# The causal mask of self-attention as rows of the operands instead of mask products and masked maxima

## What is computed

```python
x = x + _L0_attn_ref(_layernorm(x), Wq, Wk, Wv, Wo)        # causal
x = x + _L0_xattn_ref(_layernorm(x), ctx, W_kv, W_q, W_proj, b_proj)
x = x + _L0_ffn_ref(_layernorm(x), gate_w, w1, b1, w2, b2)

# inside the self-attention
attn = jnp.einsum('bhqd,bhkd->bhqk', q, k) * scale
causal = jnp.triu(jnp.ones((s, s), dtype=bool), k=1)
attn = jnp.where(causal, -jnp.inf, attn)
attn = jax.nn.softmax(attn, axis=-1)
out = jnp.einsum('bhqk,bhkd->bhqd', attn, v)
```

## Time and profile before

| | us |
|---|---|
| median of 3 runs | 183.94 |
| lowest, highest | 183.62, 191.8 |
| the profiled execution | 183.63 |
| its span, first to last instruction | 181.8 |
| PE busy | 163.6 |
| DVE busy | 129.9 |
| ACT busy | 104.9 |
| POOL busy | 67.7 |
| mean granted clock of TensorE | 0.991 |
| DMA packets, MB moved | 23329, 18.39 |

### The profile page before, as it was taken

How to read it: one execution, slowest core, us unless ns; L and a number is a source line. 1 busy time by engine, 2 the same in 40 slices (tenths; PEclk the granted TensorE clock), 3 DMA queues, 4 the chain that set the end, 5 groups by cost and what they waited for, 6 DMA issues and landing times.

```text
span 181.8 us, 4434 instructions
## 1 busy us (share of the span) xinstructions
PE 163.6 (90%) x1528; PEld 117.6 (65%) x1536; DVE 129.9 (71%) x500; ACT 104.9 (58%) x218; POOL 67.7 (37%) x132
## 2 busy tenths in 40 slices
PE   5778987979899799799999999999999998989994
PEld 4457765756666577467567556656666465879983
DVE  4488599597599879879988988999955463642110
ACT  2055531257566565665567766867746766972351
POOL 6836929178900660250232232201251071124220
PEclk9999998799999999999999999999999999999999
DMA  5914254157157245134035125104402501706400
GB/s 161 286 17 127 71 157 121 50 131 184 41 143 194 64 128 151 32 101 142 24 79 159 30 78 157 32 4 123 143 7 84 177 0 26 238 29 176 118 29 29
DMA packets 23329, 18.39 MB, mean 101 GB/s; under 512 B 2308, under 2 KB 21252, under 8 KB 22660
## 3 DMA queue, kind: packets, MB, share of 16 engines
q1 hardware_dynamic: 22552, 17.20, 34.0%
q10 hardware_dynamic: 756, 0.92, 1.8%
HBM read 12.08 MB, written 2.29 MB: 79 GB/s over the span
## 4 chain that ended last, share of the span: by engine, by line
PE 55%; DVE 23%; DMA 8%; issue 5%; SPq 3%; POOL 2%; ACT 2%; DVEq 0%; POOLq 0%; ACTq 0%
PE psV L975 11%; PE psA L929 9%; PE psB L953 8%; DVE negmax L663 8%; PE psA L1019 6%; DMA stackQ<-scratch 5%; PE psV L1036 4%; PE psM L843 4%; DMA ctx_tok<-ctx_dram 3%; DVE xn L616 3%; DVE masked L657 3%; PE psB L866 3%; PE psA L1036 2%; DVE stats L607 2%; PE psB L1019 2%
## 5 line engine op out<-in xcount | busy, mean ns | idle before, releaser
L797 ACT ACTIVATE E<-psB 128x512 f32<-128x512 f32 x112 | 62.1, 595 | 24.5 <-PE psB L958 10.2
L929 PE MATMUL psA<-stackK,stackQ 72*128 72x256 bf16 (+1 forms) x256 | 41.5, 260 | 5.1 <-DVE negmax L657 2.0
L663 DVE TENSOR_REDUCE negmax<-psA 128x2 f32<-128x512 f32 x64 | 40.6, 681 | 4.4 <-PE psA L929 4.2
L953 PE MATMUL psB<-stackQ,stackK 74*128 74x256 bf16 (+1 forms) x256 | 41.1, 259 | 0.4
L657 DVE CUSTOM_DVE_ANT_0 masked<-psA,row_mask 128x128 bf16<-128x128 f32 (+1 forms) x128 | 36.8, 347 | 6.0 <-PE psA L929 6.0
L929 PEld LDWEIGHTS psA<-stackK,stackQ 72*128 72x128 bf16 x256 | 21.7, 98 | 15.2 <-DVE negmax L663 3.0
L975 PE MATMUL psV<-E,V 128*18 128x256 f32 (+1 forms) x512 | 30.5, 356 | 0.0
L953 PEld LDWEIGHTS psB<-stackQ,stackK 74*128 74x128 bf16 x256 | 22.1, 97 | 6.7 <-ACT E L797 2.7
L513 POOL TENSOR_SCALAR rstd<-mv 128x2 f32<-128x2 f32 x12 | 2.7, 227 | 56.6 <-DVE mv L611 56.6
L975 PEld LDWEIGHTS psV<-E,V 128*18 128x18 f32 x512 | 11.9, 97 | 13.1 <-issue 6.6
L616 DVE TENSOR_SCALAR xn<-res,mv,rstd 128x128 f32<-128x128 f32 x24 | 10.0, 514 | 6.5 <-POOL rstd L514 6.4
(11 more groups left out here) (112 smaller groups left out, 249.5 us busy)
## 6 DMA issues: line engine op xcount, KB each, us to landing
stackK<-scratch SPq DMA_DIRECT2D x18, 192.0 KB
stackQ<-hid SPq DMA_DIRECT2D x36, 64.0 KB
w1s<-w_dram SPq DMA_DIRECT2D x8, 258.0 KB, 2.8
w2s<-w_dram SPq DMA_DIRECT2D x8, 256.0 KB, 4.2
stackQ<-scratch SPq DMA_DIRECT2D x2, 576.0 KB
stackK<-hid SPq DMA_DIRECT2D x16, 64.0 KB
scratch<-hid SPq DMA_DIRECT2D x4, 192.0 KB, 4.2
scratch<-parts_ctx SPq DMA_DIRECT2D x4, 192.0 KB, 6.6
```

What stands on the lines that cost most here:

```text
L663: dve.tensor_reduce(negmax[:, b, heads[0]:heads[-1] + 1:2, t], scores, AX_X, ALU.max, negate=True).then_inc(a_taken, 1)
L797: act.activation(dst, psB[:, bank].rearrange("p (h q) -> p h q", h=dst.shape[1]), ACT.Exp, scale=SCALE).then_inc(b_taken, 1)
L929: last = pe.matmul(psA[:, bank, i * keys:(i + 1) * keys], stackQ[0:ROWS, b, h, t * P:(t + 1) * P], stackK[0:ROWS, b, h, 0:keys], start=Tru ...
L953: last = pe.matmul(psB[:, bank, i * n:(i + 1) * n], stackK[:, b, h, t * P:(t + 1) * P], stackQ[:, b, h, q0:S], start=(s == 1 or i == 0), s ...
```

## The change

Each stack gets 48 more rows (CAUSAL = 120 rows in all; the first two are the rows of the maximum and of ones, of the other 46 43 are needed for a block of 128). They hold a staircase with steps of 3 tokens: the product of `kept_q` and `kept_k` rows is zero where a key may be seen and a very large negative number where not. A matmul of a diagonal block (128 queries with the same 128 keys) runs over 120 rows and so is masked; other blocks run over 72 or 74 rows as before. A matmul that held a diagonal and another block side by side is now two matmuls of 128 columns.

- First pass: the maxima of self-attention are taken by the same `tensor_reduce` as in cross-attention, one for each unit. Batches 1 to 3 use the 120 rows. Batch 0 adds a mask product on PE instead (`mask16` against the identity), one for each unit, 12 in all.
- Second pass: the mask products are gone for all four batches, the 120 rows are used.
- GpSimd makes the two constant tiles (2 memsets, 7 `affine_select`, 1 memset of two rows) where it made `mask16T`; `row_mask`, `masked` and the two DMAs of ones are gone.
- Six new DMAs of SP (`stack_keep`) spread the constants over all heads: two for batches 0 and 1 together (1.57 MB in all), two for batch 2 and two for batch 3 (0.79 MB each). They write 48 partitions, in elements of 512 bytes.
- New waits: SP's first `max_rows` and PE's first unit of batches 1 to 3 wait for these rows.

```diff
+KEPT = 48
+CAUSAL = ROWS + KEPT
+STEP = 3
...
-    start += [("stack_put", 0, 1), ("stack_fill", 0, 1)]
+    start += [("stack_put", 0, 1), ("stack_keep", 0, 0, 2), ("stack_fill", 0, 1), ("stack_keep", 0, 2, 1)]
...
     put(14, "stack_write", 0, 3, 0)
+    put(14, "stack_keep", 0, 3, 1)
...
+                if kind == "stack_keep":
+                    n = st["g"]
+                    for stack, kept in ((stackQ, kept_q), (stackK, kept_k)):
+                        sp.wait_ge(kept_set, len(KEY_STEPS) + len(QUERY_STEPS) + 1)
+                        src = kept[:, :, :].rearrange("r n q -> r (n q)").rearrange("r (o q) -> r o q", o=1)
+                        sp.dma_start(stack[ROWS:CAUSAL, b:b + n].rearrange("r b h q -> r (b h) q"),
+                                     src.to_broadcast([KEPT, n * NH, S])).then_inc(kept_in[b], 16)
...
+                    if s == 0 and b == 0:
+                        sp.wait_ge(kept_in[0], 32)
...
-                    then(pool.memset(mask16T[:, :, :], 0.0))
-                    causal(mask16T, -1)
+                    then(pool.memset(kept_k[:, :, :], KEY_TOP))
+                    then(pool.memset(kept_q[:, :, :], 0.0))
+                    stairs(kept_k, KEY_STEPS)
+                    stairs(kept_q, QUERY_STEPS)
+                    pool.memset(kept_k[0:2], 1.0).then_inc(kept_set, 1)
...
-                        for i, h in enumerate(heads):
-                            last = dve.tensor_tensor_reduce(out=masked[:, unit % 2, i * keys:(i + 1) * keys], in0=scores[:, i, 0:keys],
-                                                            in1=row_mask[:, S - keys:S], scale=-1.0, scalar=LARGEST,
-                                                            op0=ALU.add, op1=ALU.min,
-                                                            accum_out=negmax[:, b, h, t:t + 1])
+                    keys = (t + 1) * P if s == 0 else S
+                    dve.tensor_reduce(negmax[:, b, heads[0]:heads[-1] + 1:2, t], scores[:, :, 0:keys], AX_X, ALU.max, negate=True).then_inc(a_taken, 1)
...
+                    if s == 1 or b == 0:
+                        spans = [(0, keys, ROWS)]
+                    else:
+                        spans = [(k, P, CAUSAL if k == t * P else ROWS) for k in range(0, keys, P)]
+                    by_product = s == 0 and b == 0
...
+                    if by_product:
+                        blocks = psA[:, bank].rearrange("p (h k) -> p h k", h=len(heads))[:, :, t * P:(t + 1) * P]
+                        last = pe.matmul(blocks, ident16[:, :], mask16[:, 0:len(heads), :], start=False, stop=True,
+                                         skip_group_check=True)
...
-                    if s == 0:
-                        blocks = psB[:, bank].rearrange("p (h q) -> p h q", h=len(heads))[:, :, 0:P]
-                        last = pe.matmul(blocks, ident16[:, :], mask16T[:, 0:len(heads), :], start=False, stop=True,
-                                         skip_group_check=True)
+                        spans = [(q, P, CAUSAL if q == t * P else MAXROW + 2) for q in range(q0, S, P)]
```

66 lines of the change are left out of this document (34 added, 32 removed).

## The result

The change is slower; the interval leaves open whether by more than 2%. The medians are 193.96 us against 184.55 us (six timed runs each, run side by side; the change's lie between 188.19 and 200.37, those of before between 183.62 and 191.8), and the ratio is 1.028 with a 95% interval of 1.015 to 1.041. The forecast was 182.0 with a range of 178.8 to 186.0: wrong in sign, and outside the range.

The account below looks back on a forecast made before the run. SP's loop of maxima and reads was taken to bound the kernel until 59.92, the engines afterwards. Terms +0.5 + 0.1 - 1.1 - 0.7 - 0.4 = -1.6 us against 183.63 gave 182.0, range 178.8 to 186.0.

Parts of the forecast that it names:

- The bound of the kernel: Until 59.92 SP's loop of maxima and reads sets job starts, job 3 13.70 us after job 2; afterwards the engines.
- PE and VectorE: Self-attention groups: narrow matmuls at 0.057 us and plain maxima at 0.60 save each engine 0.40 us a group, 6.4 over 16.
- narrow matmuls are held to their weight load: Rival, both attention passes: 97 ns each, +0.55 us a group, +2.8 in all, 186.4 us; chance 0.06.
- Job 0's 1.3: Job 0, masked by products on PE: its maxima may come about 1.3 us earlier.
- GpSimd's selects: Making the constant tiles: seven selects cost 2.5 to 4.9 us, mostly in idle time; 0.2 taken, hidden.
- The new DMAs: 3.15 MB at 290 GB/s full share, 138 at the slow end; first two land at 23 to 29, mostly covered.
- Job 2 was to start +0.5: Start of job 2, batch 2's last read at 38.3 instead of 37.84: +0.5 us, from -1.4 to +4.
- new rows late: Rival: new rows hold up batch 1 or 2, SP's reads move 3 to 5 us; +2.3, 185.9 us; chance 0.17.
- Job 3's +0.1: Start of job 3, last two new DMAs sent while DMA engines are nearly idle: +0.1 us, 0 to +1.5.
- After 59.92: Engines set the pace: VectorE starts job 4 -1.1 us, job 4 itself -0.7, job 5 -0.4.
- VectorE stays the bound: Job 4: VectorE remains the limit and loses its waits for PE, -0.7 us (0 to -1.3).
- The clock: Rival: PE idles longer before job 3, clock halves, its first work loses 1.5 us; -0.1, 183.5 us; chance 0.10.

Follow-up runs that it names:

- products_both: Kernel before with mask products in both passes and plain maxima for all four batches, no new rows or DMAs: 186.8 us, ratio 1.023.
- products_0: Kernel before with batch 0 alone masked by products and plain maxima in the first pass: 184.3 us, ratio 1.002.
- products_01: Kernel before with batches 0 and 1 masked by products and plain maxima in the first pass: 186.4 us, ratio 1.010.
- first_pair: Kernel before plus only the first two of the six new DMAs (batches 0 and 1, 1.57 MB) and their waits: 188.6 us, ratio 1.029.
- copied: The change with its rows made by GpSimd and copied by VectorE instead of DMA, batch 0 by products in both passes: 192.0 us.
- traffic_alone: Kernel before, computing unchanged, plus six DMAs of the change's size, shape and place and its waits for them: 192.9 us, ratio 1.052.
- rows_first: The change with all six new DMAs landed before x is loaded: 218.8 us, of which 35.7 is the later start.
- ports: The change plus six DMAs of 768 KB behind its last store, to varied partitions, each alone: 6.8, 7.2, 5.0, 5.8, 5.8 and 5.3 us.
- the last four alone: Kernel before plus only the last four of the six new DMAs (batches 2 and 3, 1.57 MB): 187.0 us, ratio 1.021.
- no_mask: Kernel before with no causal mask at all: 181.8 us in its profiled execution; timed runs 185.1, 195.2 and 197.3.
- after_warm: The change with matmuls of ones added on PE where its trace showed PE idle: 195.2 us, ratio 1.050.
- dma_probe: Kernel before plus six 768 KB DMAs behind its last output, one at a time: 7.2 us into partitions 24 to 71, 4.0 with 128 partitions.
- no_mask_warm: Kernel without causal mask, plus 30 matmuls of ones on PE ahead of job 2's wait for its Q read: 182.4 us median.
- get_late: Kernel before plus the first two new DMAs, with ScalarE's read of batch 1's Q moved behind its evictions: 191.5 and 193.8 us, ratio 1.048.

## Why the prediction was wrong, and what of it held

**The bound of the kernel** was read rightly. Jobs 2 and 3 wait for SP's reads in before and in most experiments (in products_both neither does, in products_0 and products_01 job 3 does not), and a delay of the first maxima is passed on whole: 4.7 us in first_pair, 7.4 in copied.

**PE and VectorE** were right, to the row: 0.057 a narrow matmul at 120 rows, about 0.6 a maximum. The case against it, that narrow matmuls are held to their weight load or to the Trainium skill's 81 ns (TensorE: Matmul & The Clock Gate, Back-to-back issue gap), is ruled out by the rows of after. Job 0's 1.3 was right too, as products_0 and products_01 show.

**GpSimd's selects** took 1.41 for three and 2.08 for four, 3.5 us in all within the 2.5 to 4.9, and were hidden. Not foreseen: VectorE's additions beside them are slower. Its row in after, against 0.76 in before at 11.21:

```profile
12.20 0.97 DVE L650 TENSOR_TENSOR rot<-rot 128x256 f32<-128x256 f32 x2
```

In traffic_alone and rows_first, where no select runs there, it is 0.76. In the trace of after it costs some 0.2 us.

**The new DMAs are the step that failed**, in three terms of it.
First the rate. "290 GB/s at a full share from 138 at 0.48" took the share for a fraction of a limit that all transfers have in common. The fills of that row write other partitions; the keeps, alone, reach 106 to 115 GB/s with nothing beside them. The bound from below, 138 GB/s, was called the slow end and was still too fast. At the measured rate the first pair needs 13.6 us, to 31 and not to "23 to 29", and in after it lands at 25.7 and 33.0.
Second, who stands behind them. The text counted SP's queue and called batch 1's fills and read "covered if the rate is above about 150 GB/s", which it was not. It named ScalarE's read of batch 1's Q in half a sentence and gave it no price; ScalarE's write before it took 10.6 us in place of 2.0, and what is queued on ScalarE behind its own wait, `kc`, stopped PE for 5.5 us. Nor were the fills priced: SP needs 14.4 us to issue them in place of 7.5 (single issues of 4.8, 2.8 and 2.2 us with the keeps under way, mostly 0.6 in before), and everything behind them on SP, batch 2's writes and the maxima, moves with them. The Trainium skill (DMA: Bandwidth & Descriptors, section Issuing engines are not separate DMA queues) says that DMAs of all engines run on the same 16 DMA engines and interleave; the trace agrees, with the 10.6 us.
Third, the sum. Job 2 was to start +0.5, at most +4. It starts 10.2 later in after's trace (56.46 against 46.22) and 6.0 later in ports' (52.21), with most of it lost in job 0. The rival "new rows late" had the place and the sign, with a chance of 0.17, but its own price was 2.3 us; the six DMAs cost 8.4 by the medians of traffic_alone.

**Job 3's +0.1** was too small: with the last four alone jobs 1 to 3 lose 1.1, 1.0 and 1.5 us.

**After 59.92** the savings exist as forecast: 1.8 us over jobs 3 and 4 in no_mask, against 1.8. In after's trace these two jobs take 13.6 and 13.4 us where before has 14.2 and 14.2, so 1.3 comes back, and in ports' 13.3 and 13.3, which is 1.8. With the rows landed first it is nothing over the same two jobs, job 3 with a half clock of 3.4 us in it; in job 4 SP's chain of maxima, reads and nine fills takes 14.2 us and PE waits for its end. "VectorE stays the bound" in job 4 was wrong there. Why that chain is a microsecond shorter in no_mask and in ports is open.

**The clock** was a rival at 0.10, priced at 1.5 us ahead of job 3. Its stretches did come (6.8 us each at 31.5 and 55.4 in after, 10.2 at 130.4). By after_warm they are not the main cost, but the last one, with 4 to 6 us lost around it in after and ports, is more than the rival had, and in a place that no part of the forecast looked at.

**The chances**: slower by over 2% had 0.08. By the fastest run of each it is 2.5% slower, by the medians 5.1%. Both ends of the DMA term came from one kind of transfer on other partitions, and the range inherited that.

## What to carry to other kernels

Price a new transfer by a row of the same shape and the same partitions, and if there is none, keep a rate for each place apart: a share of 0.48 doesn't say that the other half can be had. Then list everything that is queued behind it, on every engine that issues DMAs, and for each what stands behind that engine's wait. And before saving work on an engine, find the loop that sets the job's length: here leaving out masking altogether gives 2.0 us in a trace and 3.0 between the fastest runs, and writing 3 MB for it cost 8.4.

## What the runs showed of the hardware

- 768 KB into 48 partitions from 72 on take 6.8 and 7.2 us, into 48 from 24 on 7.2 (with elements of 512 bytes or 16 KB), into 48 from 40 on 5.0, into 32 or 64 from 0 on 5.8, into 96 from 0 on 5.3, into 128 take 4.0 (dma_probe, ports).
- With 1.57 MB queued, issuing nine DMAs of 64 KB takes SP 14.4 us in place of 7.5, and a DMA of 192 KB that ScalarE issues takes 10.6 us in place of 2.0 (after; 10.1 to 10.3 in traffic_alone, first_pair and ports).
- VectorE's additions of 256 float32 columns from SBUF take 0.97 us for two in place of 0.76 while GpSimd runs selects (after, before).
- PE's idle times of 1.65 (no_mask_warm), 3.73 (no_mask), 5.75 (first_pair) and 7.73 us (get_late) each had a stretch at 1.2 GHz begin in or at the end of them, of 6.8, 6.8, 6.8 and 10.2 us; those of 1.93 us at 39.78 in traffic_alone and 2.62 at 42.80 in after had none. Filling the gap took the stretch away, or moved it to the next gap, and gained no time in before or in the change.
- Eight f32 products of 256 columns at the start take 1.97 us in some traces and 3.75 in others, of kernels that are the same up to there, with a granted clock of 1.00 shown in both (after and ports; before and dma_probe).
